# Causal attention of the second layer: scores formed twice, the second time key-major, in place of transposed probabilities

## The reference, cut to what matters

```python
# bias attention ("kind 0"): 16 heads of 8 channels, a bias that depends on the distance of query and key
scores = jnp.einsum('bhqd,bhkd->bhqk', q, k) * scale + _tisa_bias(amplitudes, sharpness, offsets, s)[None]
weights = jax.nn.softmax(scores, axis=-1)
attn = jnp.einsum('bhqk,bhkd->bhqd', weights, v)        # then a gated projection
# causal attention ("kind 1"): 16 heads of 8 channels, keys and values from a latent of 64
scores = jnp.where(causal, q @ k.T / sqrt(hd), -1e9)
a = jax.nn.softmax(scores, axis=-1)
out = jnp.einsum('bhqk,bkhd->bqhd', a, v)               # then Wo
# then 8 experts (128 -> 256 -> 128), all of them computed for all tokens, weighted by the top two
```

## Time and profile before

| | us |
|---|---|
| median of 3 runs (lowest, highest) | 2006.32 (2004.65, 2007.0) |
| the profiled execution, first to last instruction (its span) | 2000.4 |
| granted TensorE clock, mean | 0.954 of 2.4 GHz |
| TensorE busy | 1773.1 (89%) |
| VectorE busy | 1446.4 (72%) |
| ScalarE busy | 1013.8 (51%) |
| GpSimd busy | 832.8 (42%) |

### The profile page before, as it was taken

How to read it: one execution, slowest core, us unless ns; L and a number is a source line. 1 busy time by engine, 2 the same in 40 slices (tenths; PEclk the granted TensorE clock), 3 DMA queues, 4 the chain that set the end, 5 groups by cost and what they waited for, 6 DMA issues and landing times.

```text
span 2000.4 us, 56997 instructions
## 1 busy us (share of the span) xinstructions
PE 1773.1 (89%) x21297; PEld 1305.7 (65%) x21297; DVE 1446.4 (72%) x4539; ACT 1013.8 (51%) x1986; POOL 832.8 (42%) x1222
## 2 busy tenths in 40 slices
PE   3898889898939479999999999999999999999997
PEld 2676767677726357666677667667667667666675
DVE  6777887787731266877877877887887787778765
ACT  2554455554513146666556555655655655655542
POOL 3100111101121157667646646646646654654520
PEclk6999999999969789999999999999999999999998
DMA  4522122211018211020221221122023023021211
GB/s 118 168 81 64 34 60 78 76 46 35 7 53 277 75 48 56 31 86 26 69 78 44 64 69 57 45 64 80 25 64 101 10 67 95 14 69 46 69 38 44
DMA packets 104447, 131.74 MB, mean 66 GB/s; under 512 B 17056, under 2 KB 89184, under 8 KB 102896
## 3 DMA queue, kind: packets, MB, share of 16 engines
q1 hardware_dynamic: 72352, 98.60, 16.4%
q10 hardware_dynamic: 28496, 18.10, 3.1%
q0 software_dynamic: 3328, 11.40, 1.7%
HBM read 100.05 MB, written 28.15 MB: 64 GB/s over the span
## 4 chain that ended last, share of the span: by engine, by line
PE 51%; DVE 8%; issue 6%; POOL 2%; ACT 1%; DMA 1%; ACTq 1%; SPq 0%; POOLq 0%; DVEq 0%
PE ps L1747 16%; PE ps L1762 9%; PE ps L1733 7%; PE ps L1856 6%; PE ps L1842 5%; DVE l_X L1910 2%; PE ps L1210 2%; POOL l_Y L1593 2%; PE ps L1772 1%; PE ps L1219 1%; PE ps L1793 1%; DVE l_xn L1941 1%; ACT PT L1635 1%; PE ps L1802 1%; PE ps L1782 1%
## 5 line engine op out<-in xcount | busy, mean ns | idle before, releaser
L1593 POOL TENSOR_SCALAR l_Y<-l_X,l_nmax 128x512 f32<-128x512 f32 (+3 forms) x1024 | 676.5, 667 | 494.8 <-PE ps L1747 274.0
L1635 ACT ACTIVATE PT<-ps 128x512 f32<-128x512 f32 (+3 forms) x1024 | 519.3, 517 | 390.5 <-PE ps L1747 344.2
L1747 PE MATMUL ps<-ident,l_Y 128*128 128x128 f32 x3328 | 547.8, 279 | 12.7 <-ACT PT L1635 8.3
L1747 PEld LDWEIGHTS ps<-ident,l_Y 128*128 128x128 f32 x3328 | 386.3, 141 | 195.4 <-issue 82.9
L1910 DVE CUSTOM_DVE_ANT_0 l_X<-ps,strips 128x512 f32<-128x512 f32 x512 | 342.1, 688 | 130.6 <-PE ps L1733 127.3
L1733 PE MATMUL ps<-l_stack 72*128 72x512 bf16 (+3 forms) x1024 | 350.7, 344 | 52.2 <-DVE l_nmax L1910 40.7
L1910 DVE CUSTOM_DVE_ANT_0 l_X<-ps,mask 128x384 f32<-128x384 f32 (+3 forms) x512 | 238.2, 485 | 41.3 <-PE ps L1733 36.2
L1762 PE MATMUL ps<-PT,v_aug 128*10 128x128 f32 x6656 | 230.8, 274 | 0.0
L1762 PEld LDWEIGHTS ps<-PT,v_aug 128*10 128x10 f32 x6656 | 156.8, 91 | 71.8 <-ACT PT L1635 40.7
L1733 PEld LDWEIGHTS ps<-l_stack 72*128 72x128 bf16 x1024 | 101.9, 100 | 86.3 <-DVE l_nmax L1910 67.8
L1856 PE MATMUL ps<-l_w_e,l_hid 128*128 128x128 f32 x1024 | 141.2, 283 | 3.1 <-DVE h_tok L2105 1.7
(11 more groups left out here) (277 smaller groups left out, 2484.3 us busy)
## 6 DMA issues: line engine op xcount, KB each, us to landing
l_stack<-parts_dram SPq DMA_DIRECT2D x384, 96.0 KB
stack<-parts_dram SPq DMA_DIRECT2D x48, 384.0 KB
l_w_e<-in_L_ffn_w_dram ACTq DMA_DIRECT2D x128, 128.0 KB, 2.2
parts_dram<-l_parts SPq DMA_DIRECT2D x32, 384.0 KB, 2.5
strips<-bias_dram POOLq DMA_DIRECT2D x16, 448.0 KB, 11.5
parts_dram<-parts SPq DMA_DIRECT2D x16, 384.0 KB, 6.9
w_e<-in_L_ffn_w_dram SPq DMA_DIRECT2D x12, 256.0 KB, 5.8
marks<-marks_dram SPq DMA_DIRECT2D x48, 48.0 KB
```

What stands on the lines that cost most here:

```text
L1593: nc.gpsimd.tensor_scalar(Y[:, n % Y_BUFS, 0:w], X[:, n % X_BUFS, 0:w], -1.0, nmax[:, n % 8:n % 8 + 1], ALU.mult, ALU.add).then_inc(y_pool, 1)
L1635: nc.scalar.activation(dst, src, ACT.Exp).then_inc(moved, 1)
L1747: last = nc.tensor.transpose(ps[:, to, k * P:(k + 1) * P], Y[:, n % Y_BUFS, k * P:(k + 1) * P], ident[:])
```

## The change

In causal slots the probabilities are no longer transposed. The scores are formed twice. The first time is as before, query-major, but only for the row extremes: VectorE adds the mask in place in PSUM and keeps the minimum of the negated sum (`nmax1`). When a group's 16 tiles are done, GpSimd splits the 128 x 16 extremes into three bf16 parts (`split_max`), TensorE turns them with one matmul ("mx"), ScalarE copies them out and sends them by a DMA (`stack_max`) into three new rows of the stack (72 to 74), against rows of ones on the other side. 26 steps after its first pass each tile's scores are formed again with 75 rows, keys on the partitions (`scores_turned`): key block k against queries k x 128 to 511, so 512, 384, 256, 128 wide, and a second small matmul adds the mask of the diagonal block. The maximum is subtracted by the product itself; ScalarE takes the exponential (PT_even, PT_odd); `values_turned` multiplies four heads with one matmul each, 512 to 128 queries wide. GpSimd's subtraction is gone in causal slots.

As the second pass lags by 26 steps, and its values by 32, a causal slot's second pass ends 26 to 30 steps into the next slot. Where that is a bias slot, both kinds run side by side there. In bias slots X and Y become one buffer XY of five tiles, and `values` takes 8 tiles at a time in two calls, 256 queries wide. The transposing work takes bank 7 as a third bank while no experts run. Only 12 of 16 strips are kept; the fourth group of a bias slot is loaded during the slot (`next_strips`). The mid work comes 4 steps earlier. The experts of sequences 6 and 7 begin 19 steps later (38 steps into slot 15, and 38 after it). GpSimd's constants at the start of the layer grow by some memsets.

```diff
+HEAD_GROUPS = ((0, 1, 2, 3), (3, 1, 2, 0))
+T_LAG, B_LAG, MX_AT = 3, 26, 4
+V_AT, W_AT = 13, 32
+OUT_AT, O_AT, DIVIDE_AT, TURN_AT = (23, 46), (26, 49), (28, 51), (78, 101)
 MOE_START = {b: TILES * PLACE[1, b + 1] - 6 for b in range(B - 2)}
-MOE_START[B - 2] = TILES * PLACE[1, B - 1] + MID_AT + 1
-MOE_START[B - 1] = TILES * len(ORDER) + MID_AT + 1
+MOE_START[B - 2] = TILES * PLACE[1, B - 2] + TURN_AT[1] + 1
+MOE_START[B - 1] = TILES * PLACE[1, B - 1] + TURN_AT[1] + 1
...
-X_BUFS, Y_BUFS, PT_BUFS, W_BUFS, VW = 3, 4, 2, 3, HD + 2
+XY_BUFS, QUADS, W_BUFS, VW = 5, 3, 3, HD + 2
 GATHER_AT, PRE_AT = 40, 2
-T_LAG = 3
-SIDE, SIDE2 = 6, 7
+SIDE, SIDE2, O_BANK = 6, 7, 5
...
+def side_idle(m):
+    return not moe_at(m) and m < MOE_START[B - 1]
...
+    for a, lag in ((0, T_LAG), (1, B_LAG)):
+        if 0 <= m - lag < ALL and kind((m - lag) // TILES) == a:
+            found.append(("T", m - lag))
+    found += [("mx", k) for k in group_at(m, (m + 1, GROUP + MX_AT))]
+    found += [("O", k) for k in group_at(m, O_AT)]
+    for a in range(2):
+        k, off = divmod(m - TURN_AT[a], TILES)
+        if off == 0 and 0 <= k < SLOTS and kind(k) == a:
+            found.append(("turn", k))
...
+            at = min((3, 4, SIDE2) if side_idle(m) else (3, 4), key=lambda n: used.get(n, -1))
+            slots[what], banks[what], freed[what] = len(slots), at, used.get(at)
+            used[at] = slots[what]
...
+def values_at(m):
+    found = []
+    u, r = divmod(m - V_AT, 8)
+    if r < 2 and 0 <= u < ALL // 8 and kind(u // 8) == 0:
+        found.append((0, u, r))
+    u, r = divmod(m - W_AT, 4)
+    if r == 0 and 0 <= u < ALL // 4 and kind(u // 16) == 1:
+        found.append((1, u, 1))
+    return found
...
+def o_bank(k):
+    s, g = divmod(k, 4)
+    return SIDE if kind(s) == 1 and g >= 2 and s < SLOTS - 1 else O_BANK
...
                         sp.wait_ge(scores_ready, (s - 1) * TILES + (g + 1) * GROUP)
+                    elif s:
+                        wait_turned(sp, ("T", (s - 1) * TILES + (g + 1) * GROUP - 1))
                     for k in range(2):
                         for n in range(3):
...
+                def next_strips(s):
+                    sp.wait_ge(shifted, s * TILES + GROUP)
+                    src = bass.AP(bias_dram.tensor, head_group(s, G - 1) * 4 * 2 * T, [[1, P], [2 * T, 4], [1, STRIP]])
+                    sp.dma_start(strips[:, 0:4, :], src).then_inc(strips_next, 16)
...
-                        pool.wait_ge(turned, SLOT["T", n - Y_BUFS] + 1)
-                    nc.gpsimd.tensor_scalar(Y[:, n % Y_BUFS, 0:w], X[:, n % X_BUFS, 0:w], -1.0, nmax[:, n % 8:n % 8 + 1],
+                    nc.gpsimd.tensor_scalar(XY[:, c % XY_BUFS], XY[:, c % XY_BUFS], -1.0, nmax[:, c % 8:c % 8 + 1],
                                             ALU.mult, ALU.add).then_inc(y_pool, 1)
+                order = Chain(pool, pool_order)
...
+                def split_max(k):
+                    c = max_group(k)
+                    pool.wait_ge(shifted, (k + 1) * GROUP)
+                    if c >= 2:
+                        wait_turned(pool, ("mx", 4 * [s for s in range(SLOTS) if kind(s) == 1][(c - 2) // 4] + (c - 2) % 4))
+                    order.link(nc.gpsimd.tensor_copy(max_parts[:, c % 2, 0], nmax1[:, c % 2]))
+                    order.link(nc.gpsimd.tensor_tensor(nmax1[:, c % 2], nmax1[:, c % 2], max_parts[:, c % 2, 0], ALU.subtract))
+                    order.link(nc.gpsimd.tensor_copy(max_parts[:, c % 2, 1], nmax1[:, c % 2]))
+                    nc.gpsimd.tensor_tensor(max_parts[:, c % 2, 2], nmax1[:, c % 2], max_parts[:, c % 2, 1],
+                                            ALU.subtract).then_inc(max_split, 1)
...
+                            act.wait_ge(o_ready, UNIT[0, before] + 1)
+                        nc.scalar.activation(PT[:, quad(u, r), j], src.rearrange("p (k q) -> p k q", q=P),
+                                             ACT.Exp).then_inc(moved, 1)
+                    else:
+                        u = n // 4
+                        if j == 0 and (1, u - 2) in UNIT:
+                            act.wait_ge(o_ready, UNIT[1, u - 2] + 1)
+                        elif j == 0 and earlier(s):
+                            act.wait_ge(o_ready, UNIT[1, u - TILES // 4 - 2] + 1)
+                        nc.scalar.activation(turned_keys(q)[:, j], src[:, 0:T - q * P], ACT.Exp).then_inc(moved, 1)
                 def o_out(k):
-                    act.wait_ge(o_ready, 4 * k + 4)
-                    if k:
-                        act.wait_ge(turned, SLOT["O", k - 1] + 1)
-                    nc.scalar.copy(O_sb[:], ps[:, 5, :]).then_inc(o_evac, 1)
...
+                def stack_max(k):
+                    s, g = divmod(k, 4)
+                    wait_moved(act, ("mx", k))
+                    act.dma_start(stack[STACK:STACK + 3, 0, 4 * g:4 * (g + 1), :].rearrange("n h (q c) -> n (h q) c", c=P),
+                                  max_rows[:, max_group(k) % 2, :]).then_inc(max_stacked[g], 16)
...
+                def scores_turned(n):
+                    s, g, k, j = tile_of(n)
+                    h = 4 * g + j
+                    to = bank(("T", n))
+                    if n % GROUP == 0:
+                        pe.wait_ge(max_stacked[g], 16 * (earlier(s) + 1))
+                    nc.tensor.matmul(ps[:, to, 0:T - k * P], stack[:, 1, h, k * P:(k + 1) * P], stack[:, 0, h, k * P:T],
+                                     start=True, stop=False)
+                    nc.tensor.matmul(ps[:, to, 0:P], ident_b[:], mask_turned[:], start=False, stop=True).then_inc(turned, 1)
...
+                def values(u, r):
+                    s, g = u // 8, u // 2 % 4
+                    v = v_aug[s % 2]
+                    if r == 0:
+                        wait_moved(pe, ("T", 8 * u + 7))
+                        if u % 2 == 0:
+                            values_begin(u // 2)
+                    first, second = quad(u, 0), quad(u, 1)
+                    pair = PT[:, first:second + 1] if second > first else PT[:, first::second - first]
+                    o = ps[:, o_bank(u // 2), u % 2 * 2 * P:(u % 2 + 1) * 2 * P].rearrange("p (r q) -> p r q", q=P)
+                    for k in (2 * r, 2 * r + 1):
                         for j in range(4):
-                            last = nc.tensor.matmul(ps[32 * j:32 * j + VW, 5, q * P:(q + 1) * P], v_aug[PLACE[a, b] % 2][:, k, h + j, :],
-                                                    PT[:, unit % PT_BUFS, j, k, :], start=(k == 0), stop=(k == n - 1),
-                                                    tile_position=(0, 32 * j))
+                            last = nc.tensor.matmul(o[32 * j:32 * j + VW], v[:, k, 4 * head_group(s, g) + j, :], pair[:, :, j, k, :],
+                                                    start=(k == 0), stop=(k == TT - 1), tile_position=(0, 32 * j))
+                    if r == 1:
+                        last.then_inc(o_ready, 1)
...
+                def values_turned(u):
+                    s, g, k = u // 16, u // 4 % 4, u % 4
+                    wait_moved(pe, ("T", 4 * u + 3))
+                    if k == 0:
+                        values_begin(u // 4)
+                    for j in range(4):
+                        last = nc.tensor.matmul(ps[32 * j:32 * j + VW, o_bank(u // 4), k * P:T], v_aug[s % 2][:, k, 4 * g + j, :],
+                                                turned_keys(k)[:, j], start=(k == 0), stop=(k == TT - 1), tile_position=(0, 32 * j))
...
-                    if m % 4 == 1 and 0 <= (m - 9) // 4 < ALL // 4:
-                        values((m - 9) // 4)
+                    for a, u, r in values_at(m):
+                        if a == 0:
+                            values(u, r)
+                        else:
+                            values_turned(u)
                     for b, k in moe_at(m):
...
+                        if n % GROUP == 0 and c >= 2:
+                            dve.wait_ge(max_split, c - 1)
+                        first = T - P - q * P
+                        add = mask[:, first:T]
+                        dst, low = src, nmax1[:, c % 2, 4 * j + q:4 * j + q + 1]
                     dve.wait_ge(scores_ready, n + 1)
-                    if n >= X_BUFS:
-                        dve.wait_ge(y_pool, n - X_BUFS + 1)
-                    nc.vector.tensor_tensor_reduce(out=X[:, n % X_BUFS, 0:w], in0=ps[:, n % 3, 0:w], in1=add, scale=-1.0,
-                                                   scalar=3.0e38, op0=ALU.add, op1=ALU.min,
-                                                   accum_out=nmax[:, n % 8:n % 8 + 1]).then_inc(shifted, 1)
+                    nc.vector.tensor_tensor_reduce(out=dst, in0=src, in1=add, scale=-1.0, scalar=3.0e38, op0=ALU.add, op1=ALU.min,
+                                                   accum_out=low).then_inc(shifted, 1)
                 def divide(k):
-                    dve.wait_ge(moved, SLOT["O", k] + 1)
-                    s, g = divmod(k, G)
```

426 lines of the change are left out of this document (274 added, 152 removed).

## The result

| | before | after |
|---|---|---|
| median (lowest, highest), 4 runs each | 2006.66 (2004.65, 2012.6) | 1980.35 (1975.98, 1983.73) |
| ratio, 95% interval | | 0.9872 [0.9851, 0.9892] |
| span of the profiled execution | 2000.4 | 1974.0 |

A forecast was written before the change was run, and what follows sets the result against it. TensorE was taken to set the pace in three quarters of a slot pair, VectorE in one. Terms -1 - 8.5 + 6.4 + 3.5 - 4 - 13 + 19 + 9 = +11.4 took 2000.4 to 2011.8, median 2017; range 1973 to 2053.

The forecast's parts named there:

- where the work lands: Placing of work by slot halves: causal slot with experts -2.5 and -3.2 us, bias slot +7.0 and -0.6, pair +0.7.
- this term that I had at 0: Causal slots: removing GpSimd's 64 subtractions gives 0, since GpSimd, busy 42.3 of 82.1 us, waited for others.
- +7.0 and -0.6: Bias slot's halves: +8.2 us of overlapped work in the first, less 1.2 for the third bank; 0.6 off the second.
- rival 2: Bias slot's overlapped steps: ScalarE and banks stall each other, 6 us more in each of six slots, +36, 2053; chance 0.14.
- The clock: Causal slots with experts: two more clock falls in each of six slots, about 0.75 to 1.1 us each, +9.
- Slot 2, slot 3, slot 15 with the steps behind it: Slot 2 -8.5 us; slot 3 gets the second pass, +6.4; slot 15 -13, steps up to the last experts +19.
- Wide value products: Value products up to 512 wide take as long as narrow ones, 0; bounds 3 us a pair saved or 70 us lost.
- The write into PSUM: VectorE's causal reductions written in place in PSUM cost 0.
- the bound: VectorE's write into PSUM: 0.06 us on 512 reductions, 31 us if all on the path, due by the skill's rule.
- over 80%: Sign in bias slots' first 32 steps: ScalarE above 80% busy, TensorE full, 7 us longer.
- rival 3: Maxima's DMA comes late: TensorE stands 2 us in each of 32 groups, +32 to +60, about 2055; with rival 4 chance 0.11.
- Rival 1: Lag frees causal slots to run at VectorE's pace, 72 us each, pair gains 3.7; -28 in all, 1978; chance 0.33.
- my own sign of being wrong: Forecast is wrong if a bias slot stays below 78 us, a causal below 73, or the maxima's DMA waits exceed 5.

The follow-up runs named there:

- ring runs: Kernel before with VectorE's and GpSimd's buffers made one ring of five tiles; GpSimd's causal subtraction kept 0.9999, left out 0.9952, made but not read 1.0002.
- ring kernel: Kernel before with VectorE's three buffers and GpSimd's four made one ring of five tiles, GpSimd subtracting in place: 0.9999 of the kernel before.
- after_again: The changed kernel itself run once more, unaltered, beside other versions on the same chip: 0.9856 of the kernel before.
- e_sbuf: Changed kernel with causal reductions written to tile buffers in SBUF, not in place in PSUM: 0.9887 of the kernel before.
- b_ring_unread: Kernel before with one ring of five tiles; GpSimd's causal subtraction goes to spare buffers nobody reads, transposes read VectorE's sum: 1.0002 of the kernel before.
- lag 3: Changed kernel with the second pass 3 steps behind the first, not 26, and the maxima not subtracted: 0.9879 of the kernel before.

## Why the prediction was wrong

The forecast was +11.4 us on the profiled execution, and -26.4 came of it: of the 37.8 us between the two, 31.0 stand in the five pairs and 7.2 in slot 14. The step that failed is the causal slot with experts, in "where the work lands": its first half was to go from 43.5 to 41.0, a term of -2.5. It went to 37.0, -6.5 (38.3 with a fall), the second half to 34.9 where I had 35.4. I argued that VectorE, busy 36.9 us, would be late next, and left it 4 us of waiting. Two errors lie in that; a third term that was off is the clock's, further down.

1. **Its 36.9 us of busy time were not fixed.** GpSimd's 64 subtractions had lengthened VectorE's own operations, and I priced their removal at nothing because GpSimd waited for others. The ring runs show 1.5 us of the half and 9 us of the whole for this term that I had at 0. VectorE's busy time in the half is 37.3 us in the ring kernel, 35.1 without the subtractions and 34.3 in the changed kernel; of the last 0.8, 0.5 is a division of a group's output that falls elsewhere: two in that half before (steps 15 and 31), one after (step 12).
2. **The waits went too.** VectorE waited 6.6 us before and 2.7 after. Putting 7.7 us of work back took 3.0 of the 6.5 us away again; that is about the size I had for work. With 1.5 for GpSimd and 0.8 for the busy time that moved, about 1 us remains, if the parts may be added. I put it down to the second pass lying a whole group behind, tied to nothing that VectorE does next; no run measured it by itself.

**The bias slot: right by luck, two errors that cancel.** I had +7.0 and -0.6, measured +8.1 and -2.3, but the parts were each off. Without the bank the first half grew by 14.9 us, not 8.2. That is the stall of rival 2, of its size (6 us a bias slot), but only in the kernel without the third bank, while rival 2 was told of the one with it; that this kernel's 2043 is near its 2053 is chance, since the causal slots there took 72.0 to 73.8 us. The bank gave 6.9 in the first half, not 1.2, and 1.5 in the second, not 0.6. I priced it by the wait in the old slot, 5.7 us; it should have been priced by the wait that the overlap would cause.

**The clock.** Forecast 9 us for twelve falls. In slots 4 to 14 there were five; 6.8 us at half clock cost 1.3 to 1.7 (slots 4, 6 and 10 against slot 8), 3.4 us in slot 12 nothing; slot 14's 3.4 us has no slot to be held against. That is about 5 in all, 0.9 a fall where I had 0.75: the price was about right and the number of falls was not (`after_again` had five too). One of them:

```profile
1144.60:1147.70 3.10, 1.03 (x6) 0.38 (x4) 2.72 (x17) 1.29 (x3) 0.00 (x0) 1.00 0.01 3
1147.70:1154.50 6.80, 5.50 (x13) 2.76 (x13) 6.14 (x24) 1.39 (x3) 0.49 (x3) 0.50 0.00 0
```

The sign and what goes before it were right: TensorE busy 1.0 of 3.1 us behind VectorE's chain, then 0.5. A microsecond at half clock cost about 0.2 us here, and more in slot 10 before, from which I had my price: 1.6 us for 3.4 in the half where the fall lies (45.1 against 43.5), of which the second half gave 0.4 back. In this fall TensorE was busy 5.5 of 6.8 us, in that one 3.4 of 3.4; and 3.4 us cost 1.5 in the kernel with the bank alone, where TensorE was busy 42.3 of the half's 45.0 us. So I take it that the emptier TensorE hides part of a fall; no run varied that alone.

**What held.** Slot 2, slot 3, slot 15 with the steps behind it (net +8 against +6). Wide value products take the same time: eight passes 512 wide 1.05 us with the pipeline in it, the 32 narrow ones 1.06:

```profile
1222.41 1.05 PE L1994 MATMUL ps<-PT,v_aug 128*10 128x256 f32 x16
...
1229.16 1.05 PE L2005 MATMUL ps<-PT_even,v_aug 128*10 128x512 f32 x8
```

The write into PSUM cost nothing that the whole shows (`e_sbuf`). The Trainium skill's rule that VectorE is nearer to SBUF ("Advanced Engine Details and Errata", The Read-Write Bubble), by which the bound was due, shows in one form alone: where one in-place reduction followed another without a pause, the accumulator read began 0.648 us behind a 512 wide one (median of 43 of 128) in place of 0.609 (the other 85), 0.04 us that the time of the whole doesn't show. Not as forecast was ScalarE, 69% busy in the overlap (30.3 of 43.8) where I had over 80%. The maxima's DMA was waited for 1.7 us in all, so rival 3 was rightly small:

```profile
  DMA l_stack<-max_rows: 1.7, 4
```

**Rival 1 had the numbers, and its reason only in part.** It had 72 us a causal slot with experts (71.8 to 73.5), 3.7 a pair (3.1 to 4.7; its "five times -18" is -18 in all, 5 x 3.7), 1978 (1980.35), and my own sign of being wrong, a causal slot below 73, was met in slots 8 and 12. I gave it 0.33 and argued that TensorE stays nearly full in the second half; it did, and the slot was won in the first. But its reason was the lag and the way over VectorE and GpSimd: the way cost nothing in the old kernel with the ring (`b_ring_unread`), and of the 20 us that slots 4 to 13 gained the lag gave 6.

**Open:** why the causal slot at lag 3 takes 81 to 82 us although TensorE should have 4.9 us less to do and GpSimd is silent, and either kind of relief gave the kernel before 2 to 3.6 us a slot. Its rows narrow it down: in the first half TensorE is busy 40.8 of 43.7 us, as before (40.7) and not 2.6 less, as 80 blocks out and 32 second tiles in would make it; and VectorE waits 8.1 us, more than before (6.6), the largest part for ScalarE's activation of the experts' hidden values, 3.5 us against 1.7 before and 1.9 in the changed kernel:

```profile
DVE l_hid L2366 <- ACT l_hid L1905: 3.5, 4, 1.5
```

## What to carry to other kernels

Price a new bank or buffer by the waits of the schedule that you are about to make, not of the one you have: here one PSUM bank was worth 19 us alone, 64 us beside the overlap, and decided the sign. Before you call an engine the late one at its busy time, ask what lengthens its operations, and count work that moves to another stretch. Moving work from the stretch where one engine waits to the next saves only what the next one doesn't charge: 9 us off one slot came back as 8 on its neighbour. So read a pair of neighbours together before you call one of them won.

## What the runs showed of the hardware

- GpSimd's subtractions on SBUF lengthen some of VectorE's SBUF operations: the same 128x128 normalisation 459 ns beside them and 377 without, 341 in the changed kernel; the division's 128x128 product 583 ns and 292; but a 128x512 product 687 and 688. It made 9 us of 1996 in all, though waiting for GpSimd's result cost nothing.
- An accumulator read behind a reduction into PSUM lasts 139 ns instead of 83, but the next instruction on VectorE starts no later, unless the reduction itself followed another one into PSUM without a pause (0.04 us later).
- Of two executions of the changed kernel, one had the clock at 0.5 for 20.5 us at a stretch in slot 2, the other for 6.8 and 3.4; the slot took 53.2 and 47.5 us. 1.4 us of idle matmuls in a wait of 1.9 us kept the clock up at that place in each of slots 4 to 14, where it otherwise fell.
